# ScalarE's order in the attention loop, and the last attention's score row by way of DRAM

## The reference, cut to what matters

```python
h = relu(layernorm(x))
Wh = einsum('bnf,fo->bno', h, W)
s1, s2 = Wh @ a1, Wh @ a2
e = leaky_relu(s1[:, :, None] + s2[:, None, :], negative_slope=0.2)
attn = softmax(where(adj > 0, e, NEG_BIG), axis=-1)
x = x + elu(einsum('bij,bjo->bio', attn, Wh))
```

## Time and profile before

| | us |
|---|---|
| median of 3 runs | 1530.23 |
| lowest, highest run | 1529.61, 1532.13 |
| profiled execution | 1532.61 |
| its span, first to last instruction | 1530.8 |
| outside the span | 1.8 |
| PE busy | 1405.0 (92%) |
| DVE busy | 1136.6 (74%) |
| ACT busy | 825.4 (54%) |
| POOL busy | 380.8 (25%) |

### The profile page before, as it was taken

How to read it: one execution, slowest core, us unless ns; L and a number is a source line. 1 busy time by engine, 2 the same in 40 slices (tenths; PEclk the granted TensorE clock), 3 DMA queues, 4 the chain that set the end, 5 groups by cost and what they waited for, 6 DMA issues and landing times.

```text
span 1530.8 us, 33043 instructions
## 1 busy us (share of the span) xinstructions
PE 1405.0 (92%) x12740; PEld 1273.6 (83%) x12740; DVE 1136.6 (74%) x3270; ACT 825.4 (54%) x1825; POOL 380.8 (25%) x337
## 2 busy tenths in 40 slices
PE   5899999799945888999999999999999999999896
PEld 5899998555535777999899998989999899999785
DVE  4666664687835757888888888888888888887565
ACT  4687777022233454756656557456575665654621
POOL 6333330000010304133132231331313313223120
PEclk9999999699968998999999999999999999999988
DMA  9999992276742222131331323314223133131111
GB/s 206 230 207 210 204 215 61 96 255 231 247 155 57 61 63 72 54 97 36 104 97 43 98 58 86 99 36 109 81 61 95 37 105 91 35 83 29 42 42 43
DMA packets 109600, 161.97 MB, mean 106 GB/s; under 512 B 9472, under 2 KB 61312, under 8 KB 107392
## 3 DMA queue, kind: packets, MB, share of 16 engines
q1 hardware_dynamic: 85248, 117.86, 26.7%
q0 software_dynamic: 19584, 33.56, 12.0%
q10 hardware_dynamic: 4608, 8.39, 1.5%
HBM read 151.40 MB, written 41.94 MB: 126 GB/s over the span
## 4 chain that ended last, share of the span: by engine, by line
PE 40%; DVE 14%; ACT 6%; POOL 4%; DVEq 4%; issue 3%; DMA 0%; ACTq 0%
PE ps L1624 22%; DVE wts_A L947 4%; PE ps L1583 4%; PE ps L1606 3%; PE ps L1558 2%; POOL rs_C L852 2%; PE ps L1595 2%; DVE wts_C L947 2%; PE ps L1637 2%; PE ps L1597 2%; PE ps L1596 2%; ACT hN L1296 1%; ACT hV L1293 1%; DVEq L980 1%; PE ps L1567 1%
## 5 line engine op out<-in xcount | busy, mean ns | idle before, releaser
L1624 PE MATMUL ps<-hV,wts_B 128*128 128x129 f32 x2048 | 252.3, 279 | 11.0 <-POOL wts_B L863 4.3
L863 POOL TENSOR_TENSOR wts_B<-wts_B,off 128x1024 f32<-128x1024 f32 (+7 forms) x128 | 175.4, 1394 | 336.8 <-PE ps L1606 336.6
L1624 PEld LDWEIGHTS ps<-hV,wts_B 128*128 128x128 f32 x2048 | 243.1, 195 | 13.6 <-POOL wts_B L863 5.9
L1624 PE MATMUL ps<-hP_A,wts_A 128*128 128x129 f32 x1920 | 230.2, 275 | 0.7 <-ACT xB L1355 0.7
L1624 PEld LDWEIGHTS ps<-hP_A,wts_A 128*128 128x128 f32 x1920 | 221.6, 191 | 0.9 <-ACT xB L1355 0.9
L1624 PE MATMUL ps<-hP_C,wts_C 128*128 128x129 f32 x1920 | 220.1, 274 | 0.0
L1624 PEld LDWEIGHTS ps<-hP_C,wts_C 128*128 128x128 f32 x1920 | 217.4, 191 | 0.5
L947 DVE SCALAR_TENSOR_TENSOR wts_A<-row_A,least_A,ring_A 128x1024 f32<-128x1024 f32 x128 | 160.9, 1274 | 11.8 <-ACT row_A L1321 7.5
L294 ACT ACTIVATE maskT<-ps 128x1024 fp8e4<-128x1024 bf16 x128 | 131.3, 1026 | 55.6 <-PE ps L336 43.4
L947 DVE SCALAR_TENSOR_TENSOR wts_C<-row_C,least_C,ring_C 128x1024 f32<-128x1024 f32 x120 | 160.7, 1351 | 0.0
L348 PE MATMUL ps<-x,adj_b 128*128 128x129 f16 x896 | 121.2, 223 | 15.9 <-ACT whn L277 13.7
(11 more groups left out here) (234 smaller groups left out, 2744.3 us busy)
## 6 DMA issues: line engine op xcount, KB each, us to landing
adj_b<-in_adj POOLq DMA_DIRECT2D x120, 256.0 KB, 10.1
maskT_scratch<-maskT SPq DMA_DIRECT2D x16, 1024.0 KB, 6.8
ring_A<-maskT_scratch SPq DMA_DIRECT2D x64, 256.0 KB, 3.1
off<-maskT_scratch SPq DMA_DIRECT2D x32, 512.0 KB, 6.6
ring_C<-maskT_scratch SPq DMA_DIRECT2D x64, 256.0 KB, 3.3
xa<-in_x SPq DMA_DIRECT2D x16, 512.0 KB, 4.5
whT_scratch<-whT_s ACTq DMA_DIRECT2D x32, 256.0 KB, 6.6
whT_b<-whT_scratch SPq DMA_DIRECT2D x16, 512.0 KB, 4.8
```

The lines of the kernel that those rows point to most:

```text
L863: pool.tensor_tensor(w, w, off_fp8[:, k, k * P:N], ALU.mult).then_inc(S["B", "up"], 1)
L1624: last = nc.tensor.matmul(Q_SLOTS[c // 2 % 2][:, c % 2, 0:PW], wts[y][:, j, c * P:c * P + P], src[:, j, :], start=(j == 0), stop=(j == T - 1))
```

## The change

It has two parts, and they touch laps 2 to 15.

1. Four changes of order on ACT. `scaled("C", i-3, 3)` goes behind `relu_hT("C", ...)`; `keep_scores(i-1, 3)` goes ahead of `exps("C", i-2)`; `relu_hT("A", i+1)` goes ahead of `scale_q(i+2)`; at the lap's end `normed("C", i-1, newC, 1)` goes ahead of `scaled("C", i-2, 2)`.

2. For graphs 0 to 13 of case C the score row is made another way: PE transposes the 128 x 8 tile `us` once (`row_once`, in the place of the first half of `rows`; the second half goes), ACT takes the exponential of these 8 x 128 numbers (`store_row`, in the place of the first `row_power`; the second goes), waits for its own result and issues a DMA of the 4 KB to DRAM; SP issues a DMA that reads them back onto all 128 partitions (`load_row`, 128 times 4 KB). Graphs 14 and 15 keep the old way. The tile `us_e` lies in memory that is otherwise unused at this time, in `a_rep`.

```diff
+            us_e = {x: a_rep[0:T, k, :] for k, x in enumerate(cases)}
+            VIA = {"A": range(0), "C": range(0, B - 2)}
...
+                    def load_row(x, b):
+
+                        n = b - VIA[x].start
+                        sp.wait_ge(S[x, "s_out"], (n + 1) * 16)
+                        if b > 0:
+                            sp.wait_ge(S[x, "wts"], b * T)
+                        sp.dma_start(row_e[x][:, :], row_dram[x][n % 2].rearrange("t p -> (t p)").partition_broadcast(P)) \
+                            .then_inc(S[x, "s_in"], 16)
...
@@ SP's run
                             load_mask("A", i + 1, 1)
+                        if i - 2 in VIA["C"]:
+                            load_row("C", i - 2)
                         if 1 <= i + 2 < B:
                             load_q(i + 2)
@@ DVE's weights
-                            dve.wait_ge(S[x, "s_row"], 2 * b + 2)
+                            if b in VIA[x]:
+                                dve.wait_ge(S[x, "s_in"], (b - VIA[x].start + 1) * 16)
+                            else:
+                                dve.wait_ge(S[x, "s_row"], 2 * turned_rows(x, b) + 2)
@@ ACT
+                    def store_row(x, b):
+                        n = b - VIA[x].start
+                        act.wait_ge(S[x, "s_turned"], n + 1)
+                        if n > 0:
+                            act.wait_ge(S[x, "s_out"], n * 16)
+                        nc.scalar.activation(us_e[x], TOPS[x][0:T, :], ACT.Exp, scale=1.0 - SLOPE).then_inc(S[x, "s_kept"], 1)
+                        act.wait_ge(S[x, "s_kept"], n + 1)
+                        if n > 1:
+                            act.wait_ge(S[x, "s_in"], (n - 1) * 16)
+                        act.dma_start(row_dram[x][n % 2], us_e[x]).then_inc(S[x, "s_out"], 16)
@@ ACT's run
-                        if post:
-                            scaled("C", i - 3, 3)
...
                         if CA:
                             relu_hT("C", i - 2, "A", min(i + 1, B))
+                        if post:
+                            scaled("C", i - 3, 3)
...
                             keep_scores(i - 1, 2)
+                            keep_scores(i - 1, 3)
                         if CA:
                             exps("C", i - 2)
                         if GW:
-                            keep_scores(i - 1, 3)
...
                             keep_scores(i - 1, 7)
-                        if CA:
-                            row_power("C", i - 2, 0)
+                        if CA and i - 2 in VIA["C"]:
+                            store_row("C", i - 2)
                         if GW:
                             for j in range(1, 4):
                                 score_exps(i - 1, j)
-                        if CA:
-                            row_power("C", i - 2, 1)
...
+                        if nextA and i != 0:
+                            relu_hT("A", i + 1, "C", min(i - 1, B))
                         if 1 < i + 2 < B:
                             scale_q(i + 2)
-                        if nextA and i != 0:
-                            relu_hT("A", i + 1, "C", min(i - 1, B))
...
                             normed("C", i - 1, newC, 0)
+                        if GW:
+                            normed("C", i - 1, newC, 1)
                         if CA:
                             scaled("C", i - 2, 2)
-                        if GW:
-                            normed("C", i - 1, newC, 1)
@@ PE
+                    def row_once(x, b, free):
+
+                        n = b - VIA[x].start
+                        take(free, 1, S[x, "s_kept"], n + 1)
+                        pe.wait_ge(S[x, "us"], b + 1)
+                        nc.tensor.transpose(TOPS[x][0:T, :], us[x][:, :], ident[:, :]).then_inc(S[x, "s_turned"], 1)
@@ PE's run
                                 if j == 4:
-                                    rows("C", i - 2, free_q, 0)
+                                    if i - 2 in VIA["C"]:
+                                        row_once("C", i - 2, free_q)
...
-                            if c == c0 and CA and AA:
-                                rows("C", i - 2, free_q, 1)
```

More of the change, by code:

```diff
@@ L106, in gnn_stack_kernel @@
         pTf_dram = nc.dram_tensor("pTf_scratch", (B, P, N), fp32).ap()
+        row_dram = {x: nc.dram_tensor(f"row_scratch_{x}", (2, T, P), fp32).ap() for x in "AC"}
         NT = B * T
@@ L760, in gnn_stack_kernel @@
             S["C", "quo_exp"] = csem("C_quo_exp")
+            for x in cases:
+                for n in ("s_turned", "s_kept", "s_out", "s_in"):
+                    S[x, n] = csem(f"{x}_{n}")
             for n in ("var", "rstd", "shift", "h", "hT_made", "ahi", "lo", "gram", "kept", "lrelu", "exps", "turned", "low", "up", "tile", "rec", "quo", "done"):
@@ L788, in gnn_stack_kernel, with turned_rows @@
             TURNED = [(1, 0), (0, 0), (1, 0), (0, 0), (0, HALF), (1, 0), (1, HALF)]
+            def turned_rows(x, b):
+                return b - sum(k < b for k in VIA[x])
             def turned(k):
@@ L1316, in row_power @@
                     def row_power(x, b, h):
-                        act.wait_ge(S[x, "s_made"], 2 * b + h + 1)
+                        act.wait_ge(S[x, "s_made"], 2 * turned_rows(x, b) + h + 1)
                         y = home(x, b)
@@ L1561, in rows @@
                     def rows(x, b, free, h):
-                        take(free, 1, S[x, "s_row"], 2 * b + h + 1)
+                        take(free, 1, S[x, "s_row"], 2 * turned_rows(x, b) + h + 1)
                         if h == 0:
```

## The result

The changed kernel takes 1523.57 us (median of 5 runs, 1522.59 to 1524.63) against 1530.23 us before (here the median of 5 runs too): a ratio of 0.9955, with a 95% interval of 0.9943 to 0.9966. It is faster by 6.7 us; 15.2 us had been forecast, and the time lies above the range.

What follows compares the result with a forecast made beforehand. PE's own instructions and short stops were taken to set the lap. 12.4 us (transposes, keep_scores) plus 3.8 (normed) made 16.2, less 1.0 for peak_A: 15.2 us, 1530.23 to 1515.0; own range 1512 to 1518, chance 0.60.

Steps and rivals of the forecast that it cites:

- What bounds the kernel: PE's own instructions, 61.92 of 62.40 us in lap 8, and its few short stops set the lap.
- points 1 and 2: Laps 2 to 15: second transpose group gone, 0.44 us; copy 3 earlier in the gram stretch, 0.45; 12.4 us in all.
- point 3: Lap start: normed goes earlier, so PE's turn_h does not wait; 0.32 us in 12 laps, 3.8 us.
- point 4: ACT's scaled(C, 3) behind relu_hT, and relu_hT(A) ahead of scale_q: worth nothing.
- points 5 and 6: ACT's new work is no later; the row, by DRAM, lands 3.7 us before DVE's weights of C.
- `peak_A`: Where PE waits for DVE: DVE up to 0.1 us slower in some 12 laps, 1.0 us taken off.
- from 967.48 DVE moves with PE: Lap 8: DVE waits for PE at 967.48, 0.71 us idle, and from there follows PE's gain.
- POOL becomes the gate: Rival: PE waits 0.45 us in 12 laps for POOL at B's first weigh; 1520.4 us, chance 0.13.
- Only the transposes count: Rival: ACT's copies keep pace with PE otherwise, only seven transposes go; 10.8 us, 1519.4 us, chance 0.13.
- The row comes late: Rival: the row's trip delays DVE's weights of C; slower than before from 12.0 us on; chance 0.05.
- The clock: Rival: lap 2's granted clock of 0.72 deepens or recovers, 2 to 5 us either way; clock or order worse, chance 0.05.

Runs made afterwards that it cites:

- e4: Changed kernel with POOL's eight products of each graph cut to one column each; 1498.94 us, ratio 0.9781.
- e12: Kernel before the change with POOL's products cut to one column each; 1513.41 us, ratio 0.9885.
- e3: Kernel before with one of the four ACT orders alone: second half of normed of C ahead of scaled(C, 2); 1525.90 us, ratio 0.9964.
- e5: Changed kernel with DVE's weights of C, number 0, moved ahead of shares(A, 1); 1524.92 us, ratio 0.9963.
- e8: The changed kernel itself, run again; 1522.61 us, ratio 0.9950.
- e9: Changed kernel with DVE's columns of A, which makes peak_A, moved ahead of weights of C, number 4; 1516.40 us, ratio 0.9907.
- e1: Kernel before with the four changes of ACT's order alone, old score row; 1524.81 us, ratio 0.9953.
- e2: Changed kernel with ACT's four orders put back, so only the score row by way of DRAM; 1526.99 us, ratio 0.9980.

## Why the prediction was wrong

- **What bounds the kernel**: right. PE sets the lap, and its short stops are where something can be gained.
- **Seven transposes and `keep_scores(3)`** (points 1 and 2, 0.89 us a lap): `gram(5)` and `gram(7)` moved by 0.48 us, 0.45 forecast. The second group of transposes gave its part: PE is 0.29 us ahead at the first `weigh` of A and 0.68 behind `turn_q`, so 0.39 (0.44 forecast). But the first `weigh` of A came 0.19 us late: its slot is freed by DVE's `factors`, which ends 9.5 us into the lap in both kernels. The prediction named `factors` as a reader of `exps` and missed that PE waits for it. Together 0.68 instead of 0.89, in e4 against e12 too: a term 0.21 us too large, 2.5 us over twelve laps.
- **`normed`** (point 3, 3.8 us): right; e3's twelve laps are 4.0 us shorter than before.
- **The other two orders** (point 4): nothing was forecast. Neither was tried alone, so what they bring isn't shown.
- **ACT's new work and the row's way** (points 5 and 6): right, with room to spare. The exponential took 0.26 us (0.25), the DMA was issued 10.0 us into the lap (10.4). The small write took 1.23 us from issue to SP's next issue instead of the 3.1 I had put in from the only row at hand, so the row came 6.3 us ahead of its reader, not 3.7. The Trainium skill, page "DMA: Bandwidth & Descriptors" (section "Anatomy of one DMA — SWDGE (gpsimd) path"), puts the fixed part of a DMA started by GpSimd at about 2 us; this one, started by ScalarE, let its follower issue sooner.
- **`peak_A`** (1.0 us off in all): this is the step that failed. It was put at up to 0.1 us a lap and is 0.52 in the commonest one (0.59 against 0.07). Over the twelve laps PE's stops there sum to 6.8 us instead of 2.0, and the two other stops, in laps 6 and 8, add 1.2: 6.0 us more, where 1.0 had been taken off. Of the 14.5 us forecast for these laps, 2.5 go by points 1 and 2 and 6.0 by the stops; 6.0 are left, and 5.8 were measured. The claim "from 967.48 DVE moves with PE" was wrong: DVE was on time at that place, but its next instruction waited for a product of POOL's, and POOL doesn't follow PE. I looked for POOL's lateness at PE's first `weigh` of B, where by my sum it had 0.56 us to spare, and the pair of lengths 1.86 and 2.31, which I read as a mutual slowing, was already two instructions run one after the other: `wts_C` ends at 965.70, 1.12 us after POOL's next product starts at 964.58, and this product ends 1.19 us after `wts_C` (in e5, where nothing holds it, it takes 1.33).
- **The rivals**: "POOL becomes the gate" had the right neighbour and the wrong place; it gave 1520.4 and expected PE to wait at B's `weigh`. Only lap 6 does so. There POOL came 0.35 us late, DVE's `wts_C` took the turn first, and PE waited 0.8 us for the products. DVE in order of time in lap 6 after, then POOL:

```profile
834.99 1.28 DVE L973 SCALAR_TENSOR_TENSOR wts_C<-row_C,least_C,ring_C 128x1024 f32<-128x1024 f32 x1
```
```profile
835.19 2.49 POOL L886 TENSOR_TENSOR wts_B<-wts_B,off 128x768 f32<-128x768 f32 x1
```

  "Only the transposes count" didn't happen: `gram(5)` and `gram(7)` did move. Its sum also left out the 3.8 us of `normed` without a reason. "The row comes late" didn't happen either. "The clock" is 1.00 in full laps, as before, but in lap 2 it moved, to the better side: the stretch of the earlier trace rows, counted from the lap's start, has 0.81 instead of 0.72, and lap 2 takes 62.10 us instead of 63.40, 1.30 less where 0.89 had been forecast. e8 and e9 have 0.81 there too, and so has e3; e1 and e2 have 0.72, and their lap 2 is no more than 0.1 us shorter. What decides between the two isn't shown.

## What to carry to other kernels

When work is taken from the bounding engine, follow each of its helpers to the place where the bounding engine meets it next, and ask of every one whether its start moves too: a helper whose start is released by a third engine may not. Two instructions that are both longer than their kind in one stretch are a sign of turns, and so is an end that stays when the start moves; taking the other engine's work away, as in e4, is what settled it here. And if the gain comes out short, look for the one wait that has grown: here it was cured by moving one instruction that nobody waited for behind the one that PE needed.

## What the runs showed of the hardware

- An instruction of DVE with two inputs in SBUF and one of POOL ran one after the other but for 0.1 to 0.2 us, in either direction, with 8 columns as with 1024: 128x1024 `wts_C` took 1.28 us alone and up to 2.48 beside POOL; POOL's 128x8 power 1.64 alone and 2.67 beside DVE; even DVE's 128x8 `sf_A` 0.16 alone and 0.83 beside POOL.
- DVE's `lower`, which reads one input in PSUM and one in SBUF, was not held: those of 512 and 384 columns took 1.14 us together beside POOL's products in the changed kernel and 1.15 in e4, where no long products ran.
- A DMA of 4 KB from 8 partitions to DRAM let the next engine issue 1.21 to 1.23 us after its own issue, in all 14 graphs of the changed kernel; the read of these 4 KB onto 128 partitions landed after 3.3 to 4.9 us (median 3.8 over 14).
